# A graph kernel's edge sorts: ranks of edges from TensorE products instead of VectorE scans

## The chip, the cores and the metric

The kernel runs on one core of a Trainium2 chip. The metric is the device time of one execution in microseconds (us); several runs are taken and their median counts. TensorE (PE) multiplies matrices, PEld is its weight load, VectorE (DVE) and ScalarE (ACT) work on tiles of 128 partitions, GpSimd (POOL) here issues indirect DMAs (scatters and gathers), SyncE (SP) issues plain DMAs.

## The reference

Four graph layers share one graph of 3125 nodes with 256 features and 50000 edges: an aggregation with a softmax over incoming edges, three rounds of edge attention, a graph attention layer with 8 heads, and a rotation of the features. In this cut, `x` stands for the nodes:

```python
# layers 0 to 2 take sums over the edges, by target or by source
agg  = segment_sum(h[src] * attn_weights[:, None], tgt, N)      # layer 0, by target
proj = segment_sum(msg(Q[src], K[tgt], V[tgt], type), src, N)   # layer 1, by source, three times
out  = segment_sum(h[src] * alpha, dst, N)                      # layer 2, by target
# layer 3: one plane rotation for each edge (i, j) = (src, dst), theta = edge_weight,
# one after the other, on the rows of a 256x256 matrix; edges outside 256 change nothing
for i, j, theta in edges:
    mat[i], mat[j] = c*mat[i] - s*mat[j], s*mat[i] + c*mat[j]
x = x @ mat.T
```

Each layer's result is added to x and normalised.

## The kernel before, in words

Edges lie in tiles of 128 partitions by RT = 392. A first phase, `order_and_rotate` (names begin with `or_`), puts them in the order that the layers need and does the rotations. The layers follow, phase by phase, with a barrier of all engines between two phases. The phase does three things:

- **The list of steps.** `rotation_place` (VectorE) gives each edge with a node below 256 its rank among such edges, and all others a place far behind the end. `scatter` (GpSimd) writes one record of 16 bytes for each edge into the DRAM list `steps`, with 392 indirect DMAs of 128 rows; rows beyond the end are dropped by the DMA's bounds check.
- **Two sorts.** `sort_prepare` (VectorE) sorts edges into blocks of target nodes (DB = 100 blocks of 32, names with `d`) and then of source nodes (SB = 200 blocks of 16, names with `s`). Each block begins at a tile of 128 records. A count loop makes one instruction for each block (L152), two products on TensorE add up over partitions and nodes (`sort_offsets`), and a rank loop has three for each block: a compare that marks the block's edges (L189), a scan that counts on from the block's start (L193), and a copy under that mask into `place` (L200). Then GpSimd scatters the records of both sorts: 392 DMAs for the first (`sd_rec`), and of the second (`sb_rec`) 272 in this phase, 32 and 88 in the next two (`scatter_part`).
- **The rotations.** `rotation_fetch` (SyncE) reads steps back in batches of 256 when the whole list has been written (semaphore `listed`), and `rotation_vector`, `rotation_tensor` and `rotation_scalar` turn each batch into a matrix and multiply it in. 33 batches are fetched.

The order is set by each engine's program, written out by hand, and semaphores. VectorE's program in the phase is rotation_place, both sorts, rotation_masks, rotation_vector; GpSimd's is the scatter of steps, of `sd_rec`, of `sb_rec`. So the rotation waits for both sorts, since VectorE does these first, and for the list, and the phase ends with the later of the rotation and GpSimd's scatters.

Of the kernel before, what the change touches and what calls it, by code (L numbers as in the profile page):

```python
# [5 lines left out]
ALU = mybir.AluOpType  # L6
# [4 lines left out]
I32 = mybir.dt.int32  # L11

# [32 lines left out]
ROUND = 12582912.0  # L45

# [92 lines left out]
def sort_prepare(dve, K, B, s):  # L139

    W, T, SB, TG, full = B["W"], B["T"], B["SB"], B["TG"], [P, RT]
    i_t, blk, place, placei, rawrec, padrec, here, run = (B[n] for n in
                                                          ("i_t", "blk", "place", "placei", "rawrec", "padrec", "here", "run"))
    cnt, til, til_i, tcol, bt, bti, junk, ps_o, ps_n = (B[n] for n in
                                                        ("cnt", "til", "til_i", "tcol", "bt", "bti", "junk", "ps_o", "ps_n"))
    link = linker(dve, s["chain"])
    link(dve.tensor_scalar(i_t[:, :], B["key"][:, :], W.bit_length() - 1, None, ALU.logical_shift_right))
    link(dve.tensor_copy(blk[:, :], i_t[:, :]))
# [16 lines left out]
    for g in range(TG):  # L165
        link(dve.tensor_scalar(tcol[:, g:g + 1], K["col"][:, :], float(g * P), None, ALU.add))

    dve.wait_ge(s["offs"], 1)
    link(dve.tensor_scalar(til_i[:, 0, :], ps_n[:, 0:SB], float(P - 1), None, ALU.add))
    link(dve.tensor_scalar(til_i[:, 1, :], til_i[:, 0, :], 7, None, ALU.logical_shift_right))  # L170
    link(dve.tensor_copy(til[:, 0, :], til_i[:, 1, :]))
    link(dve.tensor_tensor_scan(til[:, 1, :], K["ones"][:, 0:1].broadcast_to([P, SB]), til[:, 0, :], 0.0,
                                ALU.mult, ALU.add))
    link(dve.tensor_tensor(til[:, 2, :], til[:, 1, :], til[:, 0, :], ALU.subtract))
    link(dve.tensor_scalar(til[:, 2, :], til[:, 2, :], float(P), -1.0, ALU.mult, ALU.add))
    link(dve.tensor_tensor(til[:, 3, :], til[:, 2, :], ps_o[:, 0:SB], ALU.add))

    for g in range(TG):
        link(dve.scalar_tensor_tensor(out=junk[:, g % 2, :], in0=til[:, 1, :], scalar=tcol[:, g:g + 1],
                                      in1=K["ones"][:, 0:1].broadcast_to([P, SB]), op0=ALU.is_le, op1=ALU.mult,  # L180
                                      accum_out=bt[:, g:g + 1]))
    dve.tensor_scalar(bti[:, :], bt[:, :], float(SB - 1), None, ALU.min).then_inc(s["tiles"], 1)

    dve.wait_ge(s["cnt"], SB)
    for k in range(SB + 2):
        if k < SB:
            if k >= 3:
                dve.wait_ge(s["put"], k - 2)
            dve.tensor_scalar(here[:, k % 3, :], blk[:, :], float(k), None, ALU.is_equal).then_inc(s["here"], 1)  # L189
        if 1 <= k < SB + 1:  # L190
            b = k - 1
            dve.wait_ge(s["here"], b + 1)
            dve.tensor_tensor_scan(run[:, b % 3, :], K["ones"][:, 0:1].broadcast_to(full), here[:, b % 3, :],  # L193
                                   til[:, 3, b:b + 1], ALU.mult, ALU.add).then_inc(s["run"], 1)
        if k >= 2:
            b = k - 2
            dve.wait_ge(s["run"], b + 1)
            if b >= 1:
                dve.wait_ge(s["put"], b)
            dve.copy_predicated(place[:, :], here[:, b % 3, :].bitcast(I32), run[:, b % 3, :]).then_inc(s["put"], 1)  # L200
    dve.wait_ge(s["put"], SB)
# [3 lines left out]
    link(dve.tensor_scalar(blk[:, :], placei[:, :], float(T), None, ALU.mult))  # L205
    link(dve.tensor_scalar(placei[:, :], i_t[:, :], 7, None, ALU.logical_shift_right))
    link(dve.tensor_tensor(placei[:, :], placei[:, :], blk[:, :], ALU.add))
    dve.sem_inc(s["placed"], 1)


def sort_offsets(pe, K, B, s):

    SB, cnt = B["SB"], B["cnt"]
    pe.wait_ge(s["cnt"], SB)
    pe.matmul(B["ps_o"][:, 0:SB], K["later"][:, :], cnt[:, :], start=True, stop=True)
    pe.matmul(B["ps_n"][:, 0:SB], K["ones"][:, :], cnt[:, :], start=True, stop=True).then_inc(s["offs"], 1)
# [13 lines left out]
def scatter(pool, rec, placei, rawrec, sc, top=None):  # L230

    for j in range(RT):
# [3 lines left out]
        if top is None:  # L236
            pool.indirect_dma_start(  # L237
                out=rec, out_offset=bass.IndirectOffsetOnAxis(ap=placei[:, j:j + 1], axis=0),
                in_=rawrec[:, j, :], in_offset=None).then_inc(sc[g % 2], 16)
        else:  # L240
            pool.indirect_dma_start(  # L241
                out=rec, out_offset=bass.IndirectOffsetOnAxis(ap=placei[:, j:j + 1], axis=0),
                in_=rawrec[:, j, :], in_offset=None, bounds_check=top, oob_is_err=False).then_inc(sc[g % 2], 16)
# [175 lines left out]
def rotation_place(dve, K, B, s):  # L419
# [403 lines left out]
def order_and_rotate(nc, K, by_target, by_source, steps, batches, M):  # L823
# [6 lines left out]
    with ExitStack() as ctx:  # L830
# [3 lines left out]
        def pb(name, shape):  # L834
# [5 lines left out]
            tot=sb("tot", [P, 2]), nbi=sb("nbi", [1, 2], I32), nbf=sb("nbf", [1, 2]), batches=batches, steps=steps, M=M,  # L840
# [9 lines left out]
        temps = dict(i_t=sb("i_t", full, I32), blk=sb("blk", full), place=sb("place", full), here=sb("here", [P, 3, RT]),  # L850
                     run=sb("run", [P, 3, RT]))
# [18 lines left out]
        with phase(nc, "or", names, K["marks"]) as (block, s):  # L870
# [31 lines left out]
            def _(dve):  # L902
                rotation_place(dve, K, B, s)
                for q, t in zip(sorts, sems):
                    sort_prepare(dve, K, q, t)
# [1447 lines left out]
```

## Time and profile before

| | |
|---|---|
| median of 3 runs | 7110.98 us (7107.94 to 7120.33) |
| the profiled execution | 7118.27 us, span 7116.5 us |
| PE, DVE, POOL, ACT busy | 61%, 72%, 60%, 17% of the span |
| the ordering phase | about 53 to 1672 us of the span |
| mean granted TensorE clock | 0.819 |

An average over the span says little here, since the phases have different limits. The profile can be asked for stages: busy time of each engine in a stretch, single instructions in order of time, and for one line of the kernel all its instructions, with the shortest, median and longest duration in ns. "Idle before" is the time for which the engine did nothing before an instruction, with what ended it. A granted clock of 1.00 is 2.4 GHz, one of 0.50 is 1.2 GHz; between them a stretch had both.

### The profile page before, as it was taken

The page shows a single profiled execution, that of the slowest core. Times are in us where ns is not written, and L with a number is a line of the kernel's source. Part 1 is how long each engine was busy: PE and PEld are TensorE (multiplying, and loading weights), DVE is VectorE, ACT ScalarE, POOL GpSimd, SP SyncE. Part 2 cuts the span into 40 slices and gives each one's busy share as a digit, 9 for nine tenths or more (in the row PEclk, how much of TensorE's full clock was granted, in tenths as well). Part 3 has the DMA queues.
Part 4 walks back from the last instruction along what each step waited for, and adds up shares of the span by engine and source line. Part 5 has one row for each costly group of instructions (what it writes and reads, how often), then busy time and mean ns, then how long its engine had stood idle before and what let it go on. Part 6 is the DMA issues. An engine that isn't in the chain of part 4 may idle for free. (4 is left out here: it accounts for less than half of the span.)

```text
span 7116.5 us, 179398 instructions
## 1 busy us (share of the span) xinstructions
PE 4316.4 (61%) x60555; PEld 3474.0 (49%) x60555; DVE 5146.7 (72%) x12108; ACT 1186.1 (17%) x2828; POOL 4288.2 (60%) x3974
## 2 busy tenths in 40 slices
PE   0000288885425554788887788886888875355541
PEld 0000166663214443677775677764777754233321
DVE  6999877776535556678774687865787855588877
ACT  0000022220011110122220122210222211222210
POOL 5888777776357760477760677741777720677720
PEclk9999999996555556999998999998999987555555
DMA  1000000001044441677722677614777500444420
GB/s 30 1 4 1 1 1 1 1 1 27 10 102 131 131 118 41 195 216 209 211 71 79 194 218 208 193 34 124 209 214 210 149 19 28 96 112 110 111 58 18
DMA packets 708570, 691.60 MB, mean 97 GB/s; under 512 B 234981, under 2 KB 589355, under 8 KB 708165
## 3 DMA queue, kind: packets, MB, share of 16 engines
q0 software_dynamic: 227328, 446.06, 22.8%
q1 hardware_dynamic: 480846, 240.51, 12.2%
q8 instruction: 218, 3.57, 0.2%
q14 instruction: 178, 1.46, 0.1%
HBM read 766.03 MB, written 77.58 MB: 119 GB/s over the span
## 5 line engine op out<-in xcount | busy, mean ns | idle before, releaser
L1671 POOL DMA_INDIRECT kvring<-kvtab,oth x1776 | 1800.9, 1014 | 821.4 <-issue 436.4
L1069 POOL DMA_INDIRECT e_hg<-htab,oth_d x992 | 1014.1, 1022 | 820.4 <-issue 764.1
L1722 PE MATMUL ea_pss<-ea_qb,ea_kT 128*128 128x128 f32 x7104 | 1016.5, 276 | 0.0
L1722 PEld LDWEIGHTS ea_pss<-ea_qb,ea_kT 128*128 128x128 f32 x7104 | 942.5, 193 | 16.0
L1766 ACT ACTIVATE ea_kT<-ea_pst 128x512 f32<-128x512 f32 x888 | 482.1, 595 | 1832.7 <-PE ea_pst L1710 1832.7
L1792 DVE TENSOR_TENSOR acc<-ea_psg,acc 128x64 f32 x1776 | 399.3, 225 | 426.6 <-PE ea_psg L1733 345.4
L1710 PE MATMUL ea_pst<-ident,kvring 128*128 128x128 f32 x3552 | 485.4, 280 | 306.8 <-DMA kvring<-kvtab,oth 304.7
L241 POOL DMA_INDIRECT steps<-or_rec,or_rplacei x392 | 566.5, 1445 | 135.7 <-issue 135.7
L1806 DVE TENSOR_REDUCE ea_sc<-ea_pss 128x64 f32<-128x1024 f32 x444 | 540.6, 1218 | 46.9 <-PE ea_pss L1722 46.9
L1710 PEld LDWEIGHTS ea_pst<-ident,kvring 128*128 128x128 f32 x3552 | 384.1, 141 | 380.6 <-DMA kvring<-kvtab,oth 217.4
L1834 DVE TENSOR_TENSOR ea_mix<-ea_hot,ea_psg 128x1024 f32<-128x1024 f32 (+1 forms) x444 | 542.2, 1221 | 0.1
L1719 PE MATMUL ea_pss<-mrow,ea_mk 128*128 128x256 bf16 x1776 | 490.2, 276 | 57.4 <-ACT ea_kT L1766 25.8
L1733 PE MATMUL ea_psg<-ea_mix,kvring 128*64 128x64 f32 x14208 | 513.9, 226 | 13.6 <-DVE ea_mix L1834 13.3
L255 POOL DMA_INDIRECT sb_rec<-srawrec,splacei x392 | 422.2, 1077 | 150.0 <-issue 121.4
L1733 PEld LDWEIGHTS ea_psg<-ea_mix,kvring 128*64 128x64 f32 x14208 | 452.6, 138 | 88.1 <-issue 84.8
L237 POOL DMA_INDIRECT sd_rec<-drawrec,dplacei x392 | 410.7, 1048 | 125.4 <-issue 123.4
L1265 DVE TENSOR_TENSOR accT<-e_psg,accT 128x96 f32 x992 | 255.0, 257 | 251.7 <-DVE accT L1265 213.2
L1196 PE MATMUL e_psg<-e_Em,e_hg 128*32 128x32 f32 x15872 | 362.4, 245 | 110.4 <-DVE e_Em L1289 109.8
L1196 PEld LDWEIGHTS e_psg<-e_Em,e_hg 128*32 128x32 f32 x15872 | 321.9, 145 | 216.8 <-DVE e_Em L1289 204.1
L1244 DVE TENSOR_REDUCE e_mt<-e_pss 32x4 f32<-32x512 f32 (+1 forms) x248 | 235.0, 948 | 184.3 <-PE e_pss L1170 183.7
L1152 PE MATMUL e_pst<-identb,e_hg 128*3 128x128 bf16 (+1 forms) x992 | 148.2, 304 | 306.7 <-DMA e_hg<-htab,oth_d 306.3
L1104 ACT ACTIVATE e_stack<-e_pst 3x512 bf16<-3x512 f32 (+1 forms) x248 | 146.1, 589 | 870.5 <-PE e_pst L1152 869.8
(506 smaller groups left out, 8321.2 us busy)
## 6 DMA issues: line engine op xcount, KB each, us to landing
ea_qb<-qtab SPq DMA_DIRECT2D x1776, 64.0 KB
qtab<-at_qst SPq DMA_DIRECT2D x75, 512.0 KB, 3.3
kvring<-kvtab,oth POOLq DMA_INDIRECT x1776
e_stack<-ohtab SPq DMA_DIRECT2D x744, 32.0 KB
kvtab<-at_kvst SPq DMA_DIRECT2D x75, 256.0 KB, 2.7
e_hg<-htab,oth_d POOLq DMA_INDIRECT x992
ea_mk<-mtab SPq DMA_DIRECT2D x444, 3.0 KB
htab<-Hd SPq DMA_DIRECT2D x2, 3200.0 KB, 11.7
```

The source lines that it names most:

```text
L241: pool.indirect_dma_start(out=rec, out_offset=bass.IndirectOffsetOnAxis(ap=placei[:, j:j + 1], axis=0), in_=rawrec[:, j, :], in_offset=Non ...
L255: pool.indirect_dma_start(out=rec, out_offset=bass.IndirectOffsetOnAxis(ap=placei[:, begin + j:begin + j + 1], axis=0), in_=rawrec[:, begi ...
L1069: pool.indirect_dma_start(out=hg[:, b % RING, u, :], out_offset=None, in_=htab, in_offset=bass.IndirectOffsetOnAxis(ap=oth[:, b * 4 + u:b ...
L1196: pe.matmul(ps_g[e % 2][h * NBD:(h + 1) * NBD, u, k, :], lhs(k * P + h * NBD, NBD), Em[:, e % 2, u, k * 4 + h if H > 1 else 0, :], start=T ...
L1671: pool.indirect_dma_start(out=kv[:, b % R, u, :], out_offset=None, in_=kvtab, in_offset=bass.IndirectOffsetOnAxis(ap=oth[:, b * QB + u:b * ...
L1710: tr = pe.transpose(ps_t[:, u, k, :], kv[:, r, u, k * P:(k + 1) * P], K["ident"][:, :])
L1719: pe.matmul(ps_s[r % 2][:, u, :], mk[:, r, u * P:(u + 1) * P], K["mrow"][:, :], start=True, stop=False, skip_group_check=True)
L1722: mm = pe.matmul(ps_s[r % 2][:, u, k * 2 * HN:(k + 1) * 2 * HN], kT[:, r % 2, u, k, :], qb[:, r, u, :], start=False, stop=True, skip_group ...
L1733: mm = pe.matmul(ps_g[r % 2][c * DH1:(c + 1) * DH1, u, :], kv[:, r, u, D + g * DH1:D + (g + 1) * DH1], mix[:, r % 2, u, g * G:(g + 1) * G, ...
L1766: ins = act.activation(kT[:, r % 2, 2 * k:2 * k + 2], ps_t[:, 2 * k:2 * k + 2], ACT.Copy)
L1806: dve.tensor_reduce(sc[:, :, :, :].rearrange("p u g h -> p (u g h)"), ps_s[r % 2][:, :, :].rearrange("p u (q n) -> p (u q) n", n=NBS), AX. ...
L1834: dve.tensor_tensor(mix[:, r % 2], hot[:, bass.ds(b * QB, QB), :].unsqueeze(2) .broadcast_to([P, QB, G * G, NBS]), ps_w[r % 2].unsqueeze(3 ...
```

## The change

The sorts get their ranks in another way. ScalarE makes for each block b a tile of max(blk + 1 − b, 0) in bf16, where blk is an edge's block (`sort_masks`, L189 after). For any blk, mask b − 2 mask b+1 + mask b+2 is 1 where blk = b and else 0. TensorE uses this twice. In the first pass (`sort_counts`, L201) weights of ones and −2 add up each mask over partitions into rows of a PSUM tile, one row for each block, which gives counts by block and column. VectorE scans these once for each 100 blocks (`sort_starts`), and TensorE adds up over blocks (`sort_firsts`). In the second pass the masks are made again, and `sort_ranks` makes five products for each block into one of two PSUM tiles: two that spread the block's starts, split into two bf16 parts, to all partitions, and three with a strictly triangular matrix that count the edges in earlier partitions. VectorE's `sort_places` has one copy for each block, under the mask blk >= b, read as 16-bit integers. Later blocks overwrite earlier ones. Masks go round a ring of 6 tiles; a mask is made when the copy six blocks back is done, and a block's products start when the copy two blocks back is done.

Steps of edges outside 256 (idle) get rows of their own behind the list, which is twice as long, and are no longer dropped by a bounds check.

```diff
-    for b in range(SB):
-        if b >= 3:
-            dve.wait_ge(s["cnt"], b - 2)
-        dve.scalar_tensor_tensor(out=run[:, b % 3, :], in0=blk[:, :], scalar=float(b),
-                                 in1=K["ones"][:, 0:1].broadcast_to(full), op0=ALU.is_equal, op1=ALU.mult,
-                                 accum_out=cnt[:, b:b + 1]).then_inc(s["cnt"], 1)
...
-            dve.tensor_scalar(here[:, k % 3, :], blk[:, :], float(k), None, ALU.is_equal).then_inc(s["here"], 1)
...
-            dve.tensor_tensor_scan(run[:, b % 3, :], K["ones"][:, 0:1].broadcast_to(full), here[:, b % 3, :],
-                                   til[:, 3, b:b + 1], ALU.mult, ALU.add).then_inc(s["run"], 1)
...
-            dve.copy_predicated(place[:, :], here[:, b % 3, :].bitcast(I32), run[:, b % 3, :]).then_inc(s["put"], 1)
...
+def sort_masks(act, B, s, t, first):
+
+    for b in range(B["SB"]):
+        n = first + b
+        if RG <= n < RG + ALLB:
+            act.wait_ge(s["used"], n - RG + 1)
+        elif n >= RG:
+            act.wait_ge(s["put"], n - RG - ALLB + 1)
+        if b == 0:
+            act.wait_ge(t["blk"], 1)
+        act.activation(B["ring"][:, n % RG, :], B["blk"][:, :], ACT.Relu, bias=B["from_b"][:, b:b + 1],
+                       scale=1.0).then_inc(s["mask"], 1)
...
+                mm = pe.matmul(B["ps_c"][h][0:RB, 0:RT], B["spike"][:, RB + 1 - r:2 * RB + 1 - r], B["ring"][:, n % RG, :],
+                               start=(r == 0), stop=(r == last), skip_group_check=True)
+        mm.then_inc(s["used"], 1)
...
+def sort_ranks(pe, B, s, t, first):
+
+    SB, ring, strict, pick = B["SB"], B["ring"], B["strict"], B["pick"]
+    pe.wait_ge(t["bases"], 1)
+    for b in range(SB):
+        n, k = first + b, first + b - ALLB
+        out = B["ps_k"][k % 2][:, 0:RT]
+        pe.wait_ge(s["mask"], min(n + 3, first + SB))
         if k >= 2:
...
+            pe.wait_ge(s["put"], k - 1)
+        h, at = b // RB, b % RB
+        pe.matmul(out, pick[0:RB, 0, at:at + 1].broadcast_to([RB, P]), B["lo"][0:RB, h, :], start=True, stop=False,
+                  skip_group_check=True)
+        pe.matmul(out, pick[0:RB, 1, at:at + 1].broadcast_to([RB, P]), B["hi"][0:RB, h, :], start=False, stop=False,
+                  skip_group_check=True)
+        for v in range(min(3, SB - b)):
+            mm = pe.matmul(out, strict[:, v % 2, :], ring[:, (n + v) % RG, :], start=False,
+                           stop=(v == min(3, SB - b) - 1), skip_group_check=True)
+        mm.then_inc(s["rank"], 1)
...
+    for b in range(B["SB"]):
+        n, k = first + b, first + b - ALLB
+        dve.wait_ge(s["rank"], k + 1)
+        if k >= 1:
+            dve.wait_ge(s["put"], k)
+        dve.copy_predicated(place[:, :], B["ring"][:, n % RG, :].bitcast(I16), B["ps_k"][k % 2][:, 0:RT]).then_inc(s["put"], 1)
...
-    link(dve.tensor_scalar(place[:, :], place[:, :], B["ps_y"][:, 0:1], -1.0 - 2.0 * P * RT, ALU.add, ALU.add))
+    idle = B["idle"]
+    dve.wait_ge(s["iota"], 3)
+    link(dve.tensor_copy(idle[:, :], B["idle_i"][:, :]))
+    link(dve.scalar_tensor_tensor(out=place[:, :], in0=place[:, :], scalar=B["ps_y"][:, 0:1], in1=idle[:, :],
+                                  op0=ALU.add, op1=ALU.subtract))
+    link(dve.tensor_scalar(place[:, :], place[:, :], -1.0, None, ALU.add))
     link(dve.tensor_tensor(place[:, :], place[:, :], act_f[:, :], ALU.mult))
-    link(dve.tensor_scalar(place[:, :], place[:, :], 2.0 * P * RT, None, ALU.add))
+    link(dve.tensor_tensor(place[:, :], place[:, :], idle[:, :], ALU.add))
...
-                scatter(pool, steps, B["placei"], B["rec"], sc[0:2], P * RT - 1)
+                scatter(pool, steps, B["placei"], B["rec"], sc[0:2])
...
+                sort_counts(pe, dsort, s, dsem, 0, range(DB))
+                sort_counts(pe, ssort, s, ssem, DB, range(MIDWAY))
+                sort_firsts(pe, K, dsort, dsem)
+                sort_counts(pe, ssort, s, ssem, DB, range(MIDWAY, SB))
+                sort_firsts(pe, K, ssort, ssem)
+                sort_ranks(pe, dsort, s, dsem, ALLB)
+                sort_ranks(pe, ssort, s, ssem, ALLB + DB)
                 rotation_tensor(pe, K, B, s)
```

On VectorE, before, the first sort's rank loop: `or_here` is the mark of a block, `or_run` the counted places, `or_dtil` the blocks' starts.

```order
L182 TENSOR_SCALAR or_dbti<-or_dbt 128x4
L189 TENSOR_SCALAR or_here<-or_blk 128x392 x2
L193 SCALAR_TENSOR_TENSOR or_run<-ones,or_dtil,or_here 128x392
L189 TENSOR_SCALAR or_here<-or_blk 128x392
L193 SCALAR_TENSOR_TENSOR or_run<-ones,or_dtil,or_here 128x392
L200 COPY_PREDICATED or_place<-or_here,or_run 128x392
```

On VectorE, now, the end of the second sort's starts and the first copies of the first sort: `or_ring` holds the masks (SBUF), `or_psr` and `or_psw` are the two PSUM tiles of ranks.

```order
L247 SCALAR_TENSOR_TENSOR or_sincl<-or_sincl,or_sbegin,or_psR 100x392 x2
L251 TENSOR_SCALAR or_near<-or_sincl 100x784
L252 TENSOR_SCALAR or_shi<-or_near 100x784
L253 SCALAR_TENSOR_TENSOR or_slo<-or_shi,or_sincl 100x784
L257 TENSOR_SCALAR or_sbti<-or_psv 128x5
L290 COPY_PREDICATED or_place<-or_ring,or_psr 128x392
L290 COPY_PREDICATED or_place<-or_ring,or_psw 128x392
```

The compares and scans are gone, and both sorts' starts now stand ahead of the first copy.

On TensorE, before, all that it had in the phase ahead of the rotation's loop:

```order
L477 MATMUL or_psy<-or_tot,later 128x1
L478 MATMUL or_psy<-or_tot,ones 128x1
L215 MATMUL or_psR<-or_dcnt,later 128x100
L216 MATMUL or_psv<-or_dcnt,ones 128x100
L215 MATMUL or_psR<-or_scnt,later 128x200
L216 MATMUL or_psw<-or_scnt,ones 128x200
```

On TensorE, now, from the counts of both sorts to the ranks of the first block; 299 more blocks like it follow.

```order
L201 MATMUL or_psm<-or_ring,or_spike 100x392 x100
L201 MATMUL or_psR<-or_ring,or_spike 100x392 x40
L212 MATMUL or_psa<-or_dtil,later 100x1
L218 MATMUL or_psa<-ones,or_dbelow 128x1 x4
L201 MATMUL or_psR<-or_ring,or_spike 100x392 x162
L212 MATMUL or_psv<-or_stil,later 100x1
L212 MATMUL or_psv<-or_stil,ones 100x1
L212 MATMUL or_psv<-or_stil,later 100x1
L218 MATMUL or_psv<-ones,or_sbelow 128x1 x10
L271 MATMUL or_psr<-or_dlo,or_pick 128x392
L273 MATMUL or_psr<-or_dhi,or_pick 128x392
L276 MATMUL or_psr<-or_ring,or_strict 128x392 x3
```

The counts and ranks of both sorts now stand on TensorE, and the starts of the first sort stand 40 blocks behind its last count.

## Rows read from the trace of the kernel before

**Rows 1.** Stages of the phase: count loop, rank loop, rotation (two stretches).
```profile
core 0: us, PE busy (x) PEld busy (x) DVE busy (x) ACT busy (x) POOL busy (x), PEclk, DMA share, GB/s
70.00:117.00 47.00, 0.00 (x0) 0.00 (x0) 47.00 (x195) 0.00 (x0) 37.18 (x33) 1.00 0.02 1
428.00:806.00 378.00, 0.00 (x0) 0.00 (x0) 371.05 (x598) 0.00 (x0) 313.48 (x200) 1.00 0.02 1
830.00:1290.00 460.00, 380.57 (x4968) 310.35 (x4966) 353.31 (x832) 98.47 (x209) 350.65 (x346) 0.94 0.03 1
1295.00:1655.00 360.00, 302.06 (x3989) 246.14 (x3989) 278.59 (x658) 80.53 (x172) 274.90 (x270) 0.94 0.03 1
```

**Rows 2.** In order of time (start us, duration us): scatters, first fetch, end of phase.
```profile
67.56 1.27 POOL L241 DMA_INDIRECT steps<-or_rec,or_rplacei  x1 [13.67 <-issue]
...
754.48 1.60 POOL L241 DMA_INDIRECT steps<-or_rec,or_rplacei  x1 [0.31 <-issue]
758.09 1.72 POOL L237 DMA_INDIRECT sd_rec<-drawrec,dplacei  x1 [2.01 <-DMA steps<-or_rec,or_rplacei]
...
823.55 7.79 SPq L810 DMA_DIRECT2D or_rec<-steps  x8
...
1655.04 1.32 POOL L255 DMA_INDIRECT sb_rec<-srawrec,splacei  x1 [0.30 <-issue]
...
1671.03 0.60 ACT L773 ACTIVATE M<-or_psm 128x512 f32<-128x512 f32 x1 [2.87 <-PE or_psm L700]
```

**Rows 3.** VectorE's block loops by line: ns min/median/max, first and last start us.
```profile
L152 DVE SCALAR_TENSOR_TENSOR or_run<-or_blk,ones x300: 564/564/568, 68.2 to 415.0; 128x392 f32<-128x392 f32 x150
...
L189 DVE TENSOR_SCALAR or_here<-or_blk x300: 333/447/505, 124.1 to 800.6; 128x392 f32<-128x392 f32 x150
...
L193 DVE TENSOR_TENSOR_SCAN or_run<-ones,or_stil,or_here x200: 1014/1016/1035, 425.4 to 802.4; 128x392 f32<-128x392 f32 x100
...
L200 DVE COPY_PREDICATED or_place<-or_here,or_run x300: 560/565/619, 126.9 to 804.0; 128x392 f32<-128x392 int32 x150
```

**Rows 4.** In order of time: scatters beside VectorE, and a gather in the attention.
```profile
76.29 1.16 POOL L241 DMA_INDIRECT steps<-or_rec,or_rplacei  x1 [0.30 <-issue]
...
421.48 0.97 POOL L241 DMA_INDIRECT steps<-or_rec,or_rplacei  x1 [0.30 <-issue]
...
812.17 0.95 POOL L237 DMA_INDIRECT sd_rec<-drawrec,dplacei  x1 [0.30 <-issue]
...
4015.43 1.22 DVE L1834 TENSOR_TENSOR ea_mix<-ea_hot,ea_psg 128x1024 f32<-128x1024 f32 x1
...
4015.48 1.00 POOL L1671 DMA_INDIRECT kvring<-kvtab,oth  x1 [0.30 <-issue]
```

**Rows 5.** ScalarE by line (ns), and two of L795 in order of time.
```profile
L470 ACT ACTIVATE or_c<-or_c,or_half_pi x1: 606/606/606, 58.2 to 58.2; 128x392 f32<-128x392 f32 x1
...
L795 ACT ACTIVATE or_R<-or_psR x64: 592/595/598, 873.1 to 1657.0; 128x512 f32<-128x512 f32 x64
...
1656.55 1.08 ACT L795 ACTIVATE or_R<-or_psR 128x512 f32<-128x512 f32 x2 [1.19 <-PE or_psR L754]
```

**Rows 6.** TensorE's bf16 products: in time, by line, and a stage's clock.
```profile
4014.77 0.27 PE L1719 MATMUL ea_pss<-mrow,ea_mk 128*128 128x256 bf16 x1
...
4014.88 0.61 PE L1722 MATMUL ea_pss<-ea_qb,ea_kT 128*128 128x128 f32 x4
...
4015.22 0.10 PEld L1719 LDWEIGHTS ea_pss<-mrow,ea_mk 128*128 128x128 bf16 x1
...
1749.97 0.83 PE L407 MATMUL tc_psh<-tc_oh_lo,tc_oh_hi 128*50 128x192 bf16 x4 [0.31 <-DVE tc_oh_lo L392]
...
L407 PEld LDWEIGHTS tc_psh<-tc_oh_lo,tc_oh_hi x392: 116/152/168, 1725.9 to 1837.4; 128*50 128x50 bf16 x196
L407 PE MATMUL tc_psh<-tc_oh_lo,tc_oh_hi x392: 355/364/368, 1725.9 to 1837.5; 128*50 128x192 bf16 x196
...
1720.00:1800.00 80.00, 54.63 (x261) 31.29 (x261) 77.41 (x137) 0.00 (x0) 63.01 (x45) 0.50 0.02 2
```

More of the change, by code:

```diff
@@ L45 @@
 ROUND = 12582912.0
+RB, RG, STEP, MIDWAY = 100, 6, 512, 40
+ALLB = DB + SB
 @contextmanager
@@ L174, in sort_prepare @@
[L174 to L181, printed above, removed]
@@ new lines, in sort_counts @@
+def sort_counts(pe, B, s, t, first, blocks):
+    for b in blocks:
+        n = first + b
+        pe.wait_ge(s["mask"], n + 1)
+        for h in range(B["H"]):
+            r, last = b - h * RB, min(RB + 1, B["SB"] - 1 - h * RB)
+            if 0 <= r <= last:
+                mm = pe.matmul(B["ps_c"][h][0:RB, 0:RT], B["spike"][:, RB + 1 - r:2 * RB + 1 - r], B["ring"][:, n % RG, :],
+                               start=(r == 0), stop=(r == last), skip_group_check=True)
+        mm.then_inc(s["used"], 1)
@@ new lines, in sort_firsts @@
+def sort_firsts(pe, K, B, s):
+    H, til, ps_t = B["H"], B["til"], B["ps_t"]
+    pe.wait_ge(s["til"], 1)
+    for h in range(H):
+        for o in range(h + 1):
+            mm = pe.matmul(ps_t[0:RB, h:h + 1], K["later" if o == h else "ones"][0:RB, 0:RB], til[0:RB, o:o + 1],
+                           start=(o == 0), stop=(o == h), skip_group_check=True)
+    mm.then_inc(s["offs"], 1)
+    pe.wait_ge(s["below"], 1)
+    for g in range(B["TG"]):
+        for h in range(H):
+            mm = pe.matmul(ps_t[:, 2 + g:3 + g], B["below"][0:RB, h, g, :], K["ones"][0:RB, 0:1], start=(h == 0),
+                           stop=(h == H - 1), skip_group_check=True)
+    mm.then_inc(s["bt"], 1)
@@ L849, in order_and_rotate @@
             ps_y=pb("psy", [P, D]))
-        temps = dict(i_t=sb("i_t", full, I32), blk=sb("blk", full), place=sb("place", full), here=sb("here", [P, 3, RT]),
-                     run=sb("run", [P, 3, RT]))
+        flat = lambda v: v.rearrange("p a b c -> p (a b c)")
+        temps = dict(i_t=sb("i_t", full, I32), place=sb("place", full), mul=sb("mul", full), ring=sb("ring", [P, RG, RT], BF16),
+                     from_b=sb("from_b", [P, SB]), spike=sb("spike", [P, 2 * RB + 1], BF16), strict=sb("strict", [P, 2, P], BF16),
+                     pick=sb("pick", [P, 2, P], BF16), near=sb("near", [P, 2, RT]),
+                     ps_k=[B["ps_r"][:, :, :].rearrange("p c n -> p (c n)"), flat(B["ps_w"][:, :, :, :])])
+        counts = [[B["ps_m"][:, :, :].rearrange("p q n -> p (q n)")], [flat(B["ps_R"][i][:, :, :, :]) for i in range(2)]]
+        small = [B["ps_a"][:, :, :].rearrange("p c n -> p (c n)"), B["ps_v"][:, :, :].rearrange("p c n -> p (c n)")]
         sorts = []
@@ L854, in order_and_rotate @@
             W, T = given["W"], given["T"]
-            SB, TG = NP // W, -(-T // P)
+            blocks, TG = NP // W, -(-T // P)
+            H = blocks // RB
             q = given["tag"]
             sorts.append(dict(
-                given, **temps, SB=SB, TG=TG,
-                padrec=sb(q + "padrec", [P, T, 2], I32), cnt=sb(q + "cnt", [P, SB]), til=sb(q + "til", [P, 4, SB]),
-                til_i=sb(q + "til_i", [P, 2, SB], I32), tcol=sb(q + "tcol", [P, TG]), bt=sb(q + "bt", [P, TG]),
-                bti=sb(q + "bti", [P, TG], I32), junk=sb(q + "junk", [P, 2, SB]),
-                ps_o=B["ps_R"][i][:, :, :, :].rearrange("p a b c -> p (a b c)"),
-                ps_n=(B["ps_w"][:, :, :, :].rearrange("p a b c -> p (a b c)") if i else
-                      B["ps_v"][:, :, :].rearrange("p a c -> p (a c)"))))
+                given, **dict(temps, near=temps["near"][:, 0:H]), SB=blocks, TG=TG, H=H, counted=DB + i * SB,
+                blk=sb(q + "blk", full), padrec=sb(q + "padrec", [P, T, 2], I32), incl=sb(q + "incl", [P, H, RT]),
+                hi=sb(q + "hi", [P, H, RT], BF16), lo=sb(q + "lo", [P, H, RT], BF16), til=sb(q + "til", [P, H]),
+                til_i=sb(q + "til_i", [P, 2, H], I32), begin=sb(q + "begin", [P, H]), upto=sb(q + "upto", [P, H]),
+                below=sb(q + "below", [P, H, TG, P]), bti=sb(q + "bti", [P, TG], I32), ps_c=counts[i], ps_t=small[i]))
+        dsort, ssort = sorts
         names = "chain chain2 chain3 chain4 S sin sins mm pads padst placed nb init listed iota"
-        names += " rec free par row l turn v vs w tt ti tl te tx tz turns r rs y ys m ms"
-        each = "chain cnt offs pads padst here run put tiles tilest placed row"
+        names += " chain5 from_b fixed mask used rank put rec free par row l turn v vs w tt ti tl te tx tz turns r rs y ys m ms"
+        each = "chain chain2 chain3 blk recs til offs below bt bases pads padst tiles tilest placed row"
         for given in (by_target, by_source):
```

143 lines of the change are left out of this document (87 added, 56 removed).

## The prediction, made before the changed kernel was run

> **What bounds the kernel now.** I first read the table of stages for the ordering phase, because the change lies in it alone. Three regimes follow each other there [rows 1]. In the count loop VectorE is busy all of 47.00 us and GpSimd gets 33 scatter DMAs through; in the rank loop VectorE is busy 371 of 378 us, GpSimd places 200 DMAs, TensorE does nothing; in the rotation TensorE is busy 83%, VectorE 77%.
>
> Then I looked at who ends the phase [rows 2]. GpSimd's first scatter starts at 67.56 and the list of steps is all issued at 756.08 (754.48 + 1.60). VectorE's rank loops end at 804.6 [rows 3]; after the tail and the rotation's masks the first fetch of steps goes out at 823.55. The last activation of the rotation ends at 1671.63. GpSimd has been done since 1656.36. So two chains end 15 us apart: VectorE's sorts plus 848.1 us of rotation (1671.63 − 823.55), and GpSimd's 1056 scatters (392 + 392 + 272). A change that shortens the first by more than 15 us hands the end to the second, and what counts is how fast GpSimd gets.
>
> Last I read what one scatter costs, by VectorE's work beside it [rows 4]. Each has 0.30 us between it and the one before. Beside the count loop it lasts 1.16, so 1.46 a piece; beside the rank loop 1.60, so 1.90; between the loops, among VectorE's short work, 0.97; without the bounds check and beside the rotation's small instructions 0.95. In the rotation the mean is (460 + 360) us / (346 + 270) = 1.331 [rows 1]. GpSimd is slowed by VectorE, not by its DMAs.
>
> **The change part by part.**
> *Removed from VectorE:* 300 counts of 0.564 us, 300 compares, 300 scans of 1.016 us. The rank loop for the sources took 425.4 to 804.6 for 200 blocks, 1.90 a block [rows 3].
>
> *Places of idle steps.* Four instructions stand for two in the rotation's placing, a CAST, two of two operands (L152's 0.564 is of that size) and a TENSOR_SCALAR (0.333 at best), about +1.1 us before GpSimd's first scatter: 68.7. All 392 scatters now write all their rows. The scatters of `sd_rec` write every row too, at 0.95 a piece, so I charge nothing, and take off nothing but 0.02 for the check.
>
> *Masks on ScalarE.* 600 activations of 128x392 with a bias from a tile. The sine of that shape and form took 0.606; two in a row on 128x512 overlapped by 0.11 (2 x 0.595 − 1.08) [rows 5]. So 0.50 to 0.61 each, I take 0.52: the 300 of the first pass end near 70.5 + 156 = 227 (221 to 253). TensorE's 302 count products are shorter at either clock (below) and are hidden by this.
>
> *Starts.* Between count and rank loop VectorE spent 10 us before (415.5 to 425.4 [rows 3]). The new part for the targets falls into ScalarE's pass; that for the sources, two scans, ten compares and some ten small ones, lies open: 12 us. Ranks start near 239.
>
> *Ranks on TensorE.* Five bf16 products of 392 columns a block. In the attention stage, with 1.00 granted (2.4 GHz), a bf16 product of 256 columns was followed by the next product's start 0.11 us later, its weight load of 0.10 hidden beside the one before [rows 6]: 0.43 ns a column, 0.17 for 392, 0.84 a block. At 0.50 granted (1.2 GHz) four of 192 columns took 0.83 with the last lasting 0.364, so 0.155 apart, 0.81 ns a column, 1.58 a block. Which level? In that 0.50 stretch TensorE was busy 54.63 of 80 us with a pause after every four products; in the rotation, at 83%, it was granted 0.94 [rows 1, 6]. The rank products run nearly without pause, so I take 2.4 GHz.
> VectorE's copy is 0.565 [rows 3] and waits for the copy before it; with signal and latency on both sides of two PSUM tiles I take 0.95 a block. 300 blocks: 285 us, to 524. The sort's tail and the rotation's masks take 19.0 as before (804.6 to 823.55): VectorE is ready at 543.
> By the Trainium skill (TensorE: Matmul & The Clock Gate, section "A second HAM failure mode: psum-queue depth-cycling") a loop that cycles PSUM banks each turn can idle just enough between its groups that the clock swings between the levels; this loop has that shape. No stretch of before shows it for such products. By it a block would cost between 0.95 and the 1.7 us of the second rival, and the gain lie between 220 and 55 us.
>
> *GpSimd's scatters.* During the first pass VectorE has next to nothing to do, so 0.95 + 0.30 = 1.26. During the ranks it does copies whose data lie in PSUM and whose mask lies in SBUF. Before has no such copy beside a scatter. The nearest row is the attention's product of an SBUF tile and a PSUM tile, 1.22 us long, beside which a gather took 1.00 [rows 4]; the far ends are the rank loop's 1.60, and 0.95. I take 0.95, as for no contention, and keep 1.60 for the range.
> The Trainium skill (SBUF — State Buffer, section "Who interferes with whom") says that a VectorE instruction with at most one SBUF input, outside the two-port modes, doesn't contend with GpSimd, and that one with two contends with what GpSimd reads. The count loop, two SBUF inputs, agrees (1.16 against 0.97); by the rule the copies would be free, and the sum stands as it is.
> 392 x 1.26 = 494, with 3 us for VectorE's short work before the first pass and between the passes: the list is issued at 68.7 + 497 = 566 and landed 2 us later (756.08 to 758.09 before): 568. The rotation thus waits 25 us for the list, no longer for VectorE, and ends at 568 + 848 = 1416. GpSimd has 664 scatters left at 1.331: 884, to 1452, less 2 us for the last 36 after the rotation's end, plus 2 to land: 1452. **GpSimd ends the phase**, 36 us after the rotation.
>
> *The sum.* 1671.6 − 1452 = 219.6. Nothing after the phase is touched but 15 more semaphores cleared on GpSimd, beside VectorE's next work. The profiled execution took 7118.3 (span 7116.5), so 6898.7; it lay 7.3 above the median of its runs, so by medians 6891; I say 6892.
>
> **The rivals.**
> *The copies hold up GpSimd.* For: VectorE writes and masks SBUF all along, and in before's rank loop the same instruction was one of three beside which a scatter took 1.60. Against: that loop also had a compare and a scan of two SBUF inputs, and PSUM-fed work left gathers at 1.00 [rows 4]. At the count loop's 1.46 a scatter 288 us of ranks pass 197 instead of 229, 32 x 1.26 = 40 us: gain 180, 6931. At 1.90: 152, 77 x 1.26 = 97: gain 123, 6988.
> *TensorE stays at 1.2 GHz.* 1.58 and some pause, 1.7 a block: ranks end at 239 + 510 = 749, fetch at 768, end at 1616: gain 55, 7056. For: the stretch at 0.50 with TensorE two thirds busy, just before the layer stages. Against: these products fill the engine more than the rotation's, granted 0.94.
> *Slower.* 1.2 GHz and every product waits for its own weights: five times 0.32 + 0.15 (a load in that slow stretch took 0.152 [rows 6]) is 2.35 a block. Ranks end at 944, fetch at 963, end at 1811: 140 us slower, 7251. It decides from the point where a block costs more than (1671.6 − 848.1 − 19 − 239)/300 = 1.89 us. Against: loads ran beside products in the attention stage.
> The change could also gain nothing if a block cost just about 1.89; I see no reason for that value.
>
> **How the numbers follow.** My forecast has 0.70, held-up scatters 0.18, TensorE at 1.2 GHz 0.06, slower 0.03, about even 0.03. The forecast's own range is 6872 to 6910: a block up to 1.15 us changes nothing, since the fetch may come 36 us after 568 before the rotation ends last, scatters of 1.00 instead of 0.95 cost up to 20, and 20 less is left for pauses that I counted twice. The range takes in the held-up scatters to the full 1.60: 6872 to 6988. A measurement here can tell 0.2%, 14 us, from no change. Faster 0.94, within 0.2% 0.03, slower 0.03.
>
> **What would show it.** In the changed profile: the first fetch at 560 to 580, released by the scatter of steps and not by VectorE; scatters of steps near 1.26 apart all along; ScalarE's mask pass at 0.50 to 0.61 each; copies 0.9 to 1.0 us apart, with 1.00 granted; the phase's end set by the last scatter of `sb_rec` near 1452, TensorE idle some 36 us before. I am wrong if scatters beside the copies last over 1.2, if copies stand over 1.2 apart, or if the rotation still ends the phase.

## The result, and the profile after

The changed kernel takes 6907.5 us (median of four runs, 6897.7 to 6908.7) against 7110.1 for the kernel before beside it: a ratio of 0.971, with a 95% interval of 0.9698 to 0.9722. The forecast was 6892, with a range of 6872 to 6988. The profiled execution took 6908.5 (span 6906.6).

The stages of the ordering phase, in the columns of [rows 1] (first pass of the masks, ranks, and two stretches of the rotation):

```profile
70.00:117.00 47.00, 46.43 (x92) 14.48 (x92) 5.22 (x16) 47.00 (x93) 35.71 (x37) 1.00 0.06 13
245.00:500.00 255.00, 252.53 (x1423) 119.09 (x1423) 172.35 (x290) 177.20 (x286) 190.78 (x199) 1.00 0.03 3
600.00:1050.00 450.00, 375.48 (x5022) 304.92 (x5022) 350.29 (x828) 101.88 (x216) 343.11 (x338) 0.95 0.03 1
1055.00:1400.00 345.00, 286.14 (x3805) 232.74 (x3805) 266.39 (x625) 77.97 (x165) 262.51 (x259) 0.95 0.03 1
```

TensorE and ScalarE now work where VectorE alone did; in the ranks TensorE is busy 252.53 of 255 us at a granted clock of 1.00, and GpSimd places 199 scatters in 255 us, where it placed 200 in 378 [rows 1]. The rotation looks as it did.

The same phase in order of time, answering [rows 2] (start, duration): first and last scatter of the steps, first fetch, first scatter of the next list, the rotation's last activation, the last scatter of the phase, and VectorE's first instruction of the next phase.

```profile
68.64 1.16 POOL L317 DMA_INDIRECT steps<-or_rec,or_rplacei  x1 [14.41 <-DVE or_rplacei L536]
...
568.87 0.96 POOL L317 DMA_INDIRECT steps<-or_rec,or_rplacei  x1 [0.30 <-issue]
571.07 1.77 SPq L891 DMA_DIRECT2D or_rec<-steps  x4
571.86 0.95 POOL L317 DMA_INDIRECT sd_rec<-drawrec,dplacei  x1 [2.03 <-DMA steps<-or_rec,or_rplacei]
...
1413.00 0.60 ACT L854 ACTIVATE M<-or_psm 128x512 f32<-128x512 f32 x1 [2.87 <-PE or_psm L781]
...
1452.90 0.96 POOL L331 DMA_INDIRECT sb_rec<-srawrec,splacei  x1 [0.30 <-issue]
1459.54 0.26 DVE L388 TENSOR_SCALAR quads<-trow_d 1x124 int32<-1x124 int32 x1 [47.76 <-PEq L59]
```

The first fetch comes with the list's landing. The rotation ends at 1413.6, GpSimd's last scatter at 1453.9, and the next phase starts 5.7 us after that. In the kernel before it started 0.3 after the last activation (1671.63 to 1671.93). What fills the 5.7 us stands among the instructions that the views do not count as work. In the changed kernel, GpSimd's DRAIN in the barrier between two phases (L59) and its clearing of semaphores (L64), by line:

```profile
L59 POOLq DRAIN  x1: 3982/3982/3982, 1455.3 to 1455.3; - x1
...
L64 POOLq EVENT_SEMAPHORE_RANGE_CLEAR  x82: 37/38/38, 1459.9 to 1465.1; - x82
```

In the kernel before, the same DRAIN:

```profile
L56 POOLq DRAIN  x1: 3982/3982/3982, 1657.8 to 1657.8; - x1
```

The last scatter lands at 1455.0, if it takes 2.1 us from its start like the others; the DRAIN holds GpSimd from 1455.3 to 1459.3, and the barrier opens behind it. The semaphores are cleared after VectorE has gone on at 1459.54. Before, the DRAIN lay beside the rotation (until 1661.8) and cost nothing.

From one start to the other it is 212.4 us; 2.6 of it is lost in later phases, so that the profiled executions differ by 209.8.

The new loops by line (ns min/median/max, first and last start), answering [rows 3, 5 and 6]:

```profile
L290 DVE COPY_PREDICATED or_place<-or_ring,or_psr x150: 592/597/606, 238.2 to 505.3; 128x392 f32<-128x392 int16 x150
...
L189 ACT ACTIVATE or_ring<-or_sblk,or_from_b x400: 604/621/623, 120.9 to 501.7; 128x392 bf16<-128x392 f32 x134
L189 ACT ACTIVATE or_ring<-or_dblk,or_from_b x200: 604/607/623, 69.7 to 322.1; 128x392 bf16<-128x392 f32 x100
...
L276 PE MATMUL or_psr<-or_ring,or_strict x448: 327/328/534, 237.0 to 504.9; 128*128 128x392 bf16 x150
...
L201 PE MATMUL or_psR<-or_ring,or_spike x202: 368/565/570, 121.6 to 225.0; 128*100 128x392 bf16 x101
```

300 blocks from 238.2 to 506.6 (the last copy starts at 506.0) are 0.89 us a block; [rows 3] had 1.90. The 300 masks of the first pass stand 0.52 apart (69.7 to 225). And this is how scatters stand beside the copies, answering [rows 4]:

```profile
394.52 0.96 POOL L317 DMA_INDIRECT steps<-or_rec,or_rplacei  x1 [0.30 <-issue]
394.52 0.60 DVE L290 COPY_PREDICATED or_place<-or_ring,or_psw 128x392 f32<-128x392 int16 x1 [0.33 <-PE or_psw L276]
...
395.78 0.96 POOL L317 DMA_INDIRECT steps<-or_rec,or_rplacei  x1 [0.30 <-issue]
```

### The profile page after: what moved, and what is told of

Its sections match the earlier page's. It is cut to its first block and busy times, and to the rows that moved or that the text cites. A ratio compares the mean times of both kernels' runs of the same rounds, so it can differ in the third digit from the quotient of the medians.

```text
span 6906.6 us, 182383 instructions
## 1 busy us (share of the span) xinstructions
PE 4719.5 (68%) x62379; PEld 3640.5 (53%) x62379; DVE 4626.0 (67%) x10912; ACT 1528.2 (22%) x3428; POOL 4085.6 (59%) x3975
## 5 line engine op out<-in xcount | busy, mean ns | idle before, releaser
L317 POOL DMA_INDIRECT steps<-or_rec,or_rplacei x392 | 376.8, 961 | 138.8 <-issue 124.3
```

The costliest lines, as they stand in the source:

```text
L317: pool.indirect_dma_start(out=rec, out_offset=bass.IndirectOffsetOnAxis(ap=placei[:, j:j + 1], axis=0), in_=rawrec[:, j, :], in_offset=Non ...
```

## The experiments

The theory: GpSimd's 1056 scatters end the phase; the sort counts only where it slows scatters or uses up its slack. Three questions follow: does each part of the change matter, does the slack exist and end where it should, and what on VectorE slows a scatter?

**Idle steps alone.** The kernel before, with the idle steps placed as in the changed kernel and no bounds check; two cuts of the edit:

```diff
-                in_=rawrec[:, j, :], in_offset=None, bounds_check=top, oob_is_err=False).then_inc(sc[g % 2], 16)
...
+            in_=rawrec[:, j, :], in_offset=None).then_inc(sc[g % 2], 16)
...
+    link(dve.scalar_tensor_tensor(out=place[:, :], in0=place[:, :], scalar=B["ps_y"][:, 0:1], in1=idle[:, :],
+                                  op0=ALU.add, op1=ALU.subtract))
```

> The kernel before with only the idle steps changed: rows of their own, no bounds check. My theory: a scatter took 1.60 us in the rank loop because of VectorE's three instructions beside it, not because of the bounds check or of rows left out, and the rotation waited for VectorE. So scatters beside the rank loop stay near 1.60 (1.55 to 1.62), those beside the count loop near 1.16, the list of steps is issued near 756, and the time stays within 10 us of before's 7110. Rival: the 1.60 came from the bounds check or from idle steps left out. Then scatters of steps fall to 0.95 to 1.0 in the rank loop and the list is issued near 570; GpSimd would be done some 180 us earlier, but the rotation still waits for VectorE's sort, so this rival too gives 7110. The scatters' duration tells the two apart, not the time.

Measured: 7097.8 us, ratio 0.9979 (0.9969 to 0.9989): 14 us faster, where I had said within 10. Scatters beside the rank loop stay near 1.6, so the bounds check is not what made them slow. But a scatter without it is 0.04 shorter there, and VectorE's block is as much shorter. The rank loop of before, and then of this kernel, in order of time:

```profile
599.81 1.01 DVE L193 TENSOR_TENSOR_SCAN or_run<-ones,or_stil,or_here 128x392 f32<-128x392 f32 x1
600.01 1.60 POOL L241 DMA_INDIRECT steps<-or_rec,or_rplacei  x1 [0.30 <-issue]
600.75 0.56 DVE L200 COPY_PREDICATED or_place<-or_here,or_run 128x392 f32<-128x392 int32 x1
601.35 0.45 DVE L189 TENSOR_SCALAR or_here<-or_blk 128x392 f32<-128x392 f32 x1
```

```profile
598.85 1.02 DVE L193 TENSOR_TENSOR_SCAN or_run<-ones,or_stil,or_here 128x392 f32<-128x392 f32 x1
599.07 1.56 POOL L236 DMA_INDIRECT steps<-or_rec,or_rplacei  x1 [0.30 <-issue]
...
600.38 0.41 DVE L189 TENSOR_SCALAR or_here<-or_blk 128x392 f32<-128x392 f32 x1
```

One scatter goes with one block: the compare starts before the scatter has ended (601.35 against 601.61) and lasts 0.45 and 0.41 instead of 0.33. The two engines wait for each other in turn, so what shortens one shortens both: from copy to copy a block of the second sort takes 1.86 us on average instead of 1.89. The first fetch moved from 823.6 to 813.8, 9.8 us; the rotation after it took 845.0 instead of 848.1, for a reason that is not shown.

**Idle steps undone.** The changed kernel with the old placing and the check. 

> The changed kernel with the idle steps as before: bounds check on, idle steps left out of the list. My theory: the masks and products carry all of the gain; the scatters of steps take 0.95 to 0.97 beside the copies, the list is issued 0 to 9 us later than 569 (392 x 0.02) and about 1 us is won back by two fewer instructions on VectorE: 6900 to 6918 against 6907.5. Rival: the bounds check makes a scatter slow. At 1.60 beside the ranks (392 scatters, about 270 of them after the first 128) the list is issued near 740, the rotation ends near 1590, GpSimd's 664 other scatters end near 1624, and the time is 7070 to 7090.

Measured: 6901.1 us, ratio 0.9704 (0.9688 to 0.972). The steps' scatters, by line:

```profile
L322 POOL DMA_INDIRECT steps<-or_rec,or_rplacei x392: 970/972/1177, 67.3 to 571.4; - x196
```

0.014 us more each, list 2.5 us later, as the theory has it. What idle rows were worth before, they are not worth beside the new sort. Its median is 6 us below the changed kernel's, with overlapping ranges. The ordering phase does not account for that: in the traces it ends 1.9 us later than in the changed kernel, and what is gained comes in later phases, which the edit leaves alone.

**One product and four products more.** In the rank loop, before the products of the masks (range(4) in the second kernel):

```diff
+        for _ in range(1):
+            pe.matmul(out, B["zero"][:, 0:P], ring[:, n % RG, :], start=False, stop=False, skip_group_check=True)
```

> The changed kernel with one product more per block in the rank loop (zero weights, so it adds nothing): six for five. My theory: TensorE sets the pace of the loop (50.00 of 50 us busy), so a block goes from 0.89 to 1.06 us and the ranks end near 557 instead of 506.6; with 19 us of tail that is 576, 5 to 8 us after the list of steps has landed at 571. The rotation's end moves from 1413.6 to about 1420, still 33 us before GpSimd's last scatter at 1453.9. The time does not change: 6900 to 6915. Rival: the phase follows the sort, and each of 300 blocks costs 0.17 us more: 6958.

> The changed kernel with four products more per block (zero weights): nine for five. My theory: a block goes to 1.50 to 1.55 us, the ranks end near 236 + 300 x 1.52 = 692, VectorE is ready and the first fetch goes out near 711, the rotation ends 842 us later near 1553 and ends the phase in GpSimd's place (1453.9, and 5.7 us until the next phase starts, of which 0.3 is left behind a rotation that ends last): the time rises by 1553 - 1459 = 94 us, to about 7002 (6985 to 7020). Scatters of steps stay at 0.95. Rival, the phase follows the sort: 300 x 0.63 = 189 us, 7096.

Measured: six products 6906.6 us (ratio 0.9708, 0.9692 to 0.9725), nine products 6996.6 us (0.9839, 0.9823 to 0.9855). The copies of the six, then of the nine:

```profile
L292 DVE COPY_PREDICATED or_place<-or_ring,or_psw x150: 592/595/604, 240.1 to 539.9; 128x392 f32<-128x392 int16 x150
```

```profile
L292 DVE COPY_PREDICATED or_place<-or_ring,or_psw x150: 592/596/602, 241.2 to 687.2; 128x392 f32<-128x392 int16 x150
```

In the nine, the first fetch and the rotation's last activation in order of time:

```profile
706.09 176.15 SPq L893 DMA_DIRECT2D or_rec<-steps  x36
...
1544.26 0.60 ACT L856 ACTIVATE M<-or_psm 128x512 f32<-128x512 f32 x1 [2.87 <-PE or_psm L783]
```

Six products lengthen the ranks by 34 us (50 expected) and the kernel by nothing. Nine lengthen them by 181, and the time rises by 89 (94 expected, 189 by the rival): the rotation now ends last, and VectorE's next phase starts at 1545.2, 0.3 after it. So a block costs nothing until the sort's slack is used up. From six to nine a product adds ((687.2 − 241.2) − (539.9 − 240.1))/298/3 = 0.164 us (298 blocks lie between the first and the last of these copies). Five would then be 0.84; the measured 0.89 has 0.05 more. The trace of the changed kernel shows why. In order of time, a copy from one PSUM tile and the next products into that tile:

```profile
301.13 0.59 DVE L290 COPY_PREDICATED or_place<-or_ring,or_psr 128x392 f32<-128x392 int16 x1 [0.35 <-PE or_psr L276]
301.26 0.66 PE L276 MATMUL or_psw<-or_ring,or_strict 128*128 128x392 bf16 x3
...
301.87 0.33 PE L271 MATMUL or_psr<-or_dlo,or_pick 100*128 100x392 bf16 x1
```

The block's first product comes 0.15 us after the copy two blocks back has ended (at 301.72), as in 290 of the 296 blocks from 240 to 505 us, and 0.07 later at the median than products that follow each other without a wait. So with five products the two PSUM tiles set the pace; with six, TensorE alone does, and the sixth costs 0.11 instead of 0.17. "TensorE sets the pace", which I had from its busy share, was not quite so.

**What slows a scatter.** Three kernels, each timed once, so that their traces count here and not their times. First the copies' data from SBUF:

```diff
-        dve.copy_predicated(place[:, :], B["ring"][:, n % RG, :].bitcast(I16), B["ps_k"][k % 2][:, 0:RT])
+        dve.copy_predicated(place[:, :], B["ring"][:, n % RG, :].bitcast(I16), B["blk"][:, :])
```

> The changed kernel, but each block's copy on VectorE takes its data from a tile in SBUF and not from the products in PSUM (the products still run and are waited for; the places are then numbered in the order of the edges, so the true places are left out). My theory: a scatter is held up by VectorE where VectorE reads two SBUF operands, as in the count loop before (1.16); so scatters beside these copies rise from 0.958 to 1.1 or more, and some 210 scatters beside the ranks cost 0.15 us each more, +30 us to the list of steps (600) and to the time, about 6935. Rival: a copy under a mask never holds up a scatter, wherever its data lie: 0.96 as before, 6907.

Measured: 6915.8 us. In order of time:

```profile
394.48 0.60 DVE L290 COPY_PREDICATED or_place<-or_ring,or_sblk 128x392 f32<-128x392 int16 x1 [0.33 <-PE or_psw L276]
394.73 1.15 POOL L317 DMA_INDIRECT steps<-or_rec,or_rplacei  x1 [0.30 <-issue]
```

A scatter that starts inside such a copy ends 0.80 after the copy (395.88 against 395.08); others stay at 0.96. The mean in the ranks is 1.03 against 0.96, and the list is issued 13 us later: the direction of the theory, at less than half the size, since only 79 of the 202 scatters beside the copies last over 1.05.

Then, beside each copy, the compare of before, and in another kernel a scan of half width:

```diff
+        dve.tensor_scalar(mul[:, :], B["blk"][:, :], float(b), None, ALU.is_equal).then_inc(s["cmp"], 1)
```

```diff
+        dve.tensor_tensor_scan(mul[:, 0:RT // 2], B["ones"][:, 0:1].broadcast_to([P, RT // 2]), B["blk"][:, 0:RT // 2], 0.0, ALU.mult, ALU.add).then_inc(s["cmp"], 1)
```

> The changed kernel with a compare more per block on VectorE, the one the rank loop had before (0.333 to 0.447 us, one SBUF operand, SBUF out), its result unused. In before this loop and the scatters kept step, one scatter of 1.60 for each block of 1.90. My theory: it is the compare that cannot run beside a scatter's last part (there it took 0.447 for 0.333, and 0.41 where the scatter was 0.04 shorter), so scatters beside it last 1.1 to 1.6 and compares over 0.35. A block then costs 1.1 to 1.2, the ranks alone would stay in their slack (up to 1.15), and the list of steps is late by 210 x 0.15 to 0.6 = 30 to 130 us: 6935 to 7030. Rival: the scan or the copy did it; then scatters stay at 0.95 to 1.0 and the time at 6907 to 6915.

> The changed kernel with a scan of half width per block more on VectorE (196 of 392 columns, some 0.5 us, its result unused), the kind the rank loop had before. My theory, that the compare held up the scatters, says: beside the scan a scatter takes 0.95 to 1.05; a block costs 1.15 to 1.2, the ranks end near 590, VectorE is ready near 609, which is 38 us after the list of steps has landed, and the rotation ends about with GpSimd: 6905 to 6925. Rival, the scan holds them up: scatters of 1.1 to 1.6 and a time of 6935 or more.

Measured: 6911.2 and 6909.7 us. With the compare, then with the scan, in order of time:

```profile
395.36 0.95 POOL L321 DMA_INDIRECT steps<-or_rec,or_rplacei  x1 [0.30 <-issue]
395.62 0.36 DVE L292 TENSOR_SCALAR or_mul<-or_sblk 128x392 f32<-128x392 f32 x1 [0.21 <-PE or_psw L276]
...
396.58 0.43 DVE L292 TENSOR_SCALAR or_mul<-or_sblk 128x392 f32<-128x392 f32 x1
396.62 0.96 POOL L321 DMA_INDIRECT steps<-or_rec,or_rplacei  x1 [0.30 <-issue]
```

```profile
397.00 0.57 DVE L292 TENSOR_TENSOR_SCAN or_mul<-ones,or_sblk 128x196 f32<-128x196 f32 x1
397.08 1.25 POOL L321 DMA_INDIRECT steps<-or_rec,or_rplacei  x1 [0.30 <-issue]
```

My theory of the compare falls: scatters beside it keep 0.96 (the longest of 249 lasts 1.01), and it is the compare that is sometimes stretched. The scan holds a scatter, which ends 0.76 after it. The rival is right in the mechanism and wrong in the price (6935 or more): only 36 of 259 scatters beside the ranks last over 1.05, since the others start just before a scan, near its end or clear of it, and the list is issued 8 us later. With a full scan of 1.01 that gives before's 1.60: the scatter of 600.01 ends at 601.61, 0.79 after the scan. By the Trainium skill (SBUF — State Buffer, section "Who interferes with whom") a VectorE instruction with two SBUF inputs contends with what GpSimd reads from SBUF, and one with at most one, outside the two-port modes, does not. The copies with their data in PSUM (0.96) and in SBUF (1.15), and the scan (1.25), agree. The same section infers that a product of two SBUF tensors leaves GpSimd's making of descriptors alone; the last experiment here measures otherwise.

**Where the scatters stand.** 40 scatters from the ordering phase to the type counts:

```diff
-PARTS = (272, 32, 88)
+PARTS = (232, 32, 128)
```

> The changed kernel with 40 scatters of the source list moved out of the ordering phase into the type counts two phases later (parts of 232, 32 and 128 instead of 272, 32 and 88). My theory: GpSimd's scatters set the end of both phases. The ordering phase then ends with the rotation's last activation (1413.6) and the next one starts 0.3 to 1 us later instead of at 1459.5: 45 us less; the type counts, where GpSimd ends last already, grow by 40 x 1.26 = 50 us. Sum +5: 6905 to 6920. Rival: the type counts or the ordering phase are not bound by GpSimd; if only the first is bound, the move gains 45 (6862), if only the second, it loses 50 (6957).

Measured: 6903.3 us, ratio 0.9706 (0.969 to 0.9722), 2 below the range expected. In the trace the ordering phase ends with the rotation, and the next starts 0.3 later:

```profile
1413.11 0.60 ACT L854 ACTIVATE M<-or_psm 128x512 f32<-128x512 f32 x1 [2.87 <-PE or_psm L781]
```

```profile
L388 DVE TENSOR_SCALAR quads<-trow_d x1: 256/256/256, 1414.0 to 1414.0; 1x124 int32<-1x124 int32 x1
```

It is 45.5 us earlier than 1459.5, and the type counts' last scatter starts at 1658.4 instead of 1651.6. The phase after them starts 1.0 us later than in the changed kernel (1662.4 against 1661.4) and not 6.8, since GpSimd's DRAIN there took 1.36 us instead of 7.24. GpSimd bounds both phases; what is taken from one is paid in the other, but for the DRAIN.

**Scatters where GpSimd is idle.** A version to beat both kernels:

```diff
-PARTS = (272, 32, 88)
+PARTS = (232, 32, 64, 24, 24, 16)
...
+                        C=D + 1, bias=K["b0"], rest=rest, part=3)
+                layer0_nodes(nc, K, Hd[:, :, :], tmp0[:, :, :], maglog, p0, q0, p3, htab, ad0, rest, 4)
...
+                dense(nc, "win", K, K["X"], io["Win"], io["b_in"], Hd, rest=rest, part=5)
+                sort_tables(nc, K, "sb", TS, NBS, recs_s, oth, kl, trow_s, pairs, mtab=mtab)
```

> The changed kernel with the source list's scatters moved to where GpSimd has nothing to do: 232 in the ordering phase (272), 32 beside the target tables, 64 in the type counts (88), 24 beside layer 0's projection, 24 beside its node tables, 16 beside the projection that opens the second layer, and the source tables built after that. My theory: GpSimd ends the ordering phase and the type counts, and nothing waits for it in the three later places. The ordering phase ends 45 us earlier, as with parts of 232, 32 and 128; the type counts end with VectorE's and SyncE's work, 30 us earlier than 1661; 24 scatters of 1.26 (30 us) lie under a projection of 35 us, 24 under 50 us of VectorE's work, and 16 under another projection; three more phase ends with semaphores and rings to clear cost 2 us each. 45 + 30 - 6 = 69 us: 6838 (6825 to 6860). Rival: scatters hold up VectorE and ScalarE in the projections, or the phase ends cost more; if all 64 moved scatters are paid for at 1.3, 83 us, the time is 6907 or above.

Measured: 6849.2 us, inside the range expected, where the kernel before took 7134.2 on that chip: ratio 0.9598 (0.9585 to 0.9611). Against the changed kernel's 0.971 that is 1.2% less, some 80 us; the two were timed on different chips, and the medians as they stand differ by 58. In the traces the same work, the source tables included, is done 68 us earlier (the attention's first product starts at 2542.2 instead of 2610.1), where 69 had been forecast; the phases after that, which the edit leaves alone, take 10 us longer in this trace. The node tables of layer 0 in order of time:

```profile
1635.12 6.82 DVE L2110 TENSOR_REDUCE st<-tmp 128x25 f32<-128x6400 f32 x1
...
1641.30 0.96 POOL L331 DMA_INDIRECT sb_rec<-srawrec,splacei  x1 [0.30 <-issue]
...
1642.07 6.82 DVE L2112 TENSOR_TENSOR tmp<-Hd,att 128x6400 f32<-128x6400 f32 x1
...
1642.56 7.15 POOL L331 DMA_INDIRECT sb_rec<-srawrec,splacei  x1 [0.30 <-issue]
1648.92 6.82 DVE L2113 TENSOR_REDUCE st<-tmp 128x25 f32<-128x6400 f32 x1
1650.02 0.96 POOL L331 DMA_INDIRECT sb_rec<-srawrec,splacei  x1 [0.30 <-issue]
```

Beside a reduction, one operand, five scatters pass at 0.96 or 0.97 each; beside a product of two SBUF tensors one scatter lasts 7.15 and ends 0.82 after it.

## Why the prediction was right, step by step

- *First scatter* 68.7: 68.64. *Masks* 0.52 apart, first pass to 227: 0.52, last count product at 225.0. *Ranks start* 239: 238.2.
- *A block* 0.95: 0.89. *Ranks end* 524: 506.6. The step held, two PSUM tiles between TensorE and VectorE's copy, and its 0.06 too much cost nothing, since the list of steps came later. The clock was 1.00 as taken, the loads (0.096 us) lay beside products; the rivals of the slow clock and of open weight loads fall. The loop that cycles two PSUM tiles kept its clock, with 2.5 us of TensorE's 255 idle. The Trainium skill's warning of such loops (TensorE: Matmul & The Clock Gate, section "A second HAM failure mode: psum-queue depth-cycling") did not come true here.
- *Scatters beside the copies* 0.95: 0.958 at the median. This was the step with the widest bounds, and the rival with 0.18 on it falls; that its mechanism exists is shown by the copies from SBUF.
- *List landed* 568: 571.1. The 392 scatters took 501 us, not 497. Three pauses, which the forecast has not, cost 5.1 us: before the scatters at 213.29, 356.64 and 500.41 GpSimd stood still for 1.68, 1.69 and 2.66 us instead of 0.30. VectorE's short work cost less than the 3 us charged. *Rotation ends* 1416: 1413.6, since it took 842.5 us, not 848.1; why is not shown (from 838.8 to 848.1 in this case's traces).
- *GpSimd ends the phase* at 1452: its scatters of the two sorts began at 571.9 instead of 568 and took 882 us, as forecast (884 less 2). The last landed at 1455.0, 1.1 after its end and not 2.
- *The sum* 219.6: 212.4 at the next phase's start. The mis-sized term is the phase's end, for which I charged nothing beyond the landing. The clearing of semaphores, which I put beside VectorE's next work, does lie there. What I had no term for is GpSimd's DRAIN, 3.98 of the 4.5 us between landing and the next start. It is hidden when the rotation ends last (0.3 us before, with nine products and with 232 scatters) and not when GpSimd does. 3.9 − 0.9 + 4.5 − 0.3 = 7.2 is the whole difference.
- The rest of the 15.5 us between 6892 and 6907.5: 2.6 in later phases, and 5.7 from setting the forecast 7 below the profiled execution, as before's median stood; the changed kernel's stood only 1.0 below. These parts add up and cancel nothing, and 6907.5 lies near the upper end of the forecast's own range (6910).

One thing in the working was too simple though its number held: "GpSimd is slowed by VectorE". They hold each other up, and by the kind of operand, which is why the idle rows moved the first fetch by 9.8 us in the old kernel and by 2.5 in the new.

## What to carry to other kernels

When one chain is shortened, work out what ends second and by how much; here 15 us of cover made GpSimd the bound, and the gain (212 us) was set by its scatters, not by the 298 us by which the ranks ended earlier. Then ask where that engine has nothing to do: 64 scatters moved from the ordering phase and the type counts under projections and node tables brought another 68 us in the traces. If GpSimd's scatters are the last to end in a phase, charge the DRAIN behind them too (3.98 us here).

## What the runs showed of the hardware

- A scatter DMA on GpSimd that starts while VectorE runs an instruction with two SBUF operands ends 0.76 to 0.84 us after that instruction: beside a scan of 1.01 us it took 1.60, beside a product of 6.82 us 7.15. One that starts in the last 0.1 us of such an instruction just takes its 0.96. Scatters that started 0.04 and 0.16 us before a scan kept 0.95 and 0.96. Which part of a scatter needs the other's access is not settled.
- Beside reductions, compares and copies under a mask with data in PSUM a scatter mostly keeps 0.95 to 0.97, though a compare may be stretched from 0.33 to 0.45.
- In the loop of before this locked the two engines in step, one scatter of 1.60 to one block of 1.89; with scatters 0.04 us shorter the block was 1.86.
- GpSimd's DRAIN at the end of a phase took, by the number of scatters in the phase (changed kernel and the last two experiments): 16, 1.36 us; 24, 2.01; 32, 2.67; 64, 5.28; 88, 7.24, so some 0.08 for each. But it took 1.36 after 128, 0.72 after 1016 and 3.98 after 1056, as if for 16, 8 and 48. The pauses in the list of steps tell of the same count: the first came behind the 113th scatter, the others 112 and 224 scatters later, and 128, 1016 and 1056 are 16, 8 and 48 above a multiple of 112. What GpSimd does in the pauses and in the DRAIN is not shown. The scatter behind the first pause:

```profile
213.29 0.97 POOL L317 DMA_INDIRECT steps<-or_rec,or_rplacei  x1 [1.68 <-issue]
```

- The count pass lost its clock. Stretches of TensorE in the changed kernel (busy, granted clock, DMA share, GB/s), two of the count pass and one of the ranks:

```profile
120.00:150.00 30.00, 28.65 (x67) 1.00 0.03 2
...
200.00:225.00 25.00, 25.00 (x50) 0.50 0.03 2
...
260.00:300.00 40.00, 39.93 (x226) 1.00 0.03 3
```

  TensorE shows itself busy throughout, with a product every 0.52 us in the first two, and was granted 1.00 (2.4 GHz), then 0.50 (1.2 GHz), then 1.00 again from 239.8, some 3 us into the rank products. It cost nothing: the count products last 0.565 us at either level and ScalarE's masks hide them.
- 392-column bf16 products at a granted clock of 1.00 follow each other every 0.164 us, which is 0.42 ns a column (0.43 was taken from [rows 6]).
